# Gated cross-attention block with an expert router: VectorE turns the updated rows in 32x32 blocks, transfers within SBUF place them, and the batch chain runs a unit later

## The reference, cut to what matters

```
x = x + tanh(g_xattn) * attention(layernorm(x), ctx)     # Wq, Wk: 256x512, Wv: 256x512, Wo: 512x256
h = layernorm(x)                                         # over the 2048 positions of a row
logits = h @ router_weight.T + router_bias               # [rows, 2048] x [2048, 64]
scores = softmax(logits);  w, idx = top_k(scores, 8)
out = h * sum(w) + dense(w, idx) @ expert_bias           # [rows, 64] x [64, 2048]
x = x + tanh(g_ffn) * out
```

## Time and profile before

| | us |
|---|---|
| median of three runs | 1318.22 |
| lowest, highest | 1317.71, 1319.21 |
| span of the profiled execution (first to last instruction) | 1316.7 |
| TensorE products busy in it | 1273.2 |
| VectorE busy | 1004.8 |
| ScalarE busy | 893.3 |
| GpSimd busy | 712.7 |
| DMA queue of SyncE, share of the 16 engines | 27.7% |

### The profile page before, as it was taken

The page is one execution under the profiler, slowest core; times in us unless marked ns, Lnnn a source line. Parts: engine busy times, 40 slices in busy tenths (PEclk is TensorE's granted clock), DMA queues, the critical chain, the costliest instruction groups (busy, mean ns, idle before and its releaser), DMA issues.

```text
span 1316.7 us, 37880 instructions
## 1 busy us (share of the span) xinstructions
PE 1273.2 (97%) x15313; PEld 1120.4 (85%) x15313; DVE 1004.8 (76%) x1871; ACT 893.3 (68%) x1600; POOL 712.7 (54%) x662
## 2 busy tenths in 40 slices
PE   3999999999999999999999999999999999999997
PEld 3898888889878889798887899878888798888875
DVE  6669768896788966888678776888768797687677
ACT  4676667677686676766667776676676766686755
POOL 2655664556645665456663655636664556654531
PEclk9999999999999999999999999999999999999999
DMA  9331111811136111451115411153111721123103
GB/s 277 110 104 43 34 42 51 262 40 39 43 102 216 36 39 35 149 170 43 34 43 165 154 32 42 34 192 128 43 35 38 242 78 43 34 78 114 34 6 128
DMA packets 120620, 116.15 MB, mean 88 GB/s; under 512 B 11392, under 2 KB 88320, under 8 KB 120320
## 3 DMA queue, kind: packets, MB, share of 16 engines
q1 hardware_dynamic: 119584, 113.74, 27.7%
q10 hardware_dynamic: 864, 0.01, 0.0%
HBM read 80.06 MB, written 33.65 MB: 86 GB/s over the span
## 4 chain that ended last, share of the span: by engine, by line
PE 84%; DVE 7%; ACT 5%; issue 2%; DMA 1%; POOL 0%; SPq 0%; DVEq 0%; ACTq 0%; POOLq 0%
PE ring L316 9%; PE ring L317 8%; PE ring L318 8%; PE ring L436 5%; PE ring L392 4%; PE ring L403 4%; PE ring L438 4%; PE ring L437 4%; PE ring L355 4%; PE ring L331 4%; PE ring L332 4%; PE ring L333 4%; PE ring L417 4%; PE ring L451 4%; PE PR L463 3%; ACT X L720 2%
## 5 line engine op out<-in xcount | busy, mean ns | idle before, releaser
L316 PE MATMUL ring<-z_hi,wqk_hi 128*128 128x256 f32 x1024 | 297.1, 290 | 21.8 <-DVE z_lo L1029 21.8
L1128 POOL TENSOR_TENSOR cx_lo<-cx,cx_hi 128x512 fp32r<-128x512 f32 x128 | 165.9, 1296 | 262.7 <-ACT cx_hi L640 262.7
L317 PE MATMUL ring<-z_hi,wqk_lo 128*128 128x256 f32 x1024 | 290.5, 284 | 0.0
L318 PE MATMUL ring<-z_lo,wqk_hi 128*128 128x256 f32 x1024 | 290.3, 283 | 0.0
L316 PEld LDWEIGHTS ring<-z_hi,wqk_hi 128*128 128x128 f32 x1024 | 197.1, 193 | 32.8 <-DVE wqk_lo L1004 21.8
L851 DVE SCALAR_TENSOR_TENSOR xt<-ring,cst,mg 128x256 f32<-128x256 f32 x256 | 112.0, 478 | 144.2 <-PE ring L438 144.2
L1122 POOL TENSOR_TENSOR z_lo<-z,z_hi 128x1024 fp32r<-128x1024 f32 x62 | 148.5, 2394 | 134.7 <-ACT z_hi L624 134.7
L835 DVE RECIPROCAL o<-ring 128x512 f32<-128x512 f32 x64 | 214.1, 3345 | 0.4 <-PE ring L403 0.4
L317 PEld LDWEIGHTS ring<-z_hi,wqk_lo 128*128 128x128 f32 x1024 | 197.3, 193 | 0.0
L318 PEld LDWEIGHTS ring<-z_lo,wqk_hi 128*128 128x128 f32 x1024 | 197.2, 193 | 0.0
L1134 POOL TENSOR_TENSOR X<-X,xt 128x512 f32<-128x512 f32 x128 | 163.7, 1282 | 42.6 <-DVE xt L851 32.1
(11 more groups left out here) (154 smaller groups left out, 3032.1 us busy)
## 6 DMA issues: line engine op xcount, KB each, us to landing
cx<-in_ctx SPq DMA_DIRECT2D x128, 256.0 KB, 2.7
out_y<-X SPq DMA_DIRECT2D x128, 256.0 KB, 3.0
X<-in_x SPq DMA_DIRECT2D x112, 256.0 KB, 5.2
mg<-in_mask SPq DMA_DIRECT2D x64, 128.0 KB, 3.0
X<-in_x SPq DMA_DIRECT2D x8, 512.0 KB, 7.5
sel<-rows_d SPq DMA_DIRECT2D x256, 3.0 KB
X<-in_eb SPq DMA_DIRECT2D x2, 512.0 KB, 7.9
X<-in_wqT SPq DMA_DIRECT2D x1, 512.0 KB, 6.1
```

Of the source, the lines that this page charges most:

```text
L316: e.matmul(o, wqk_hi[:, t, cols], z_hi[:, t, :], t == 0, False)
L317: e.matmul(o, wqk_lo[:, t, cols], z_hi[:, t, :], False, False)
L318: last = e.matmul(o, wqk_hi[:, t, cols], z_lo[:, t, :], False, t == DT - 1)
L1128: e.tensor_tensor(cx_lo[:], cx[p % NC][:], f32(cx_hi[:]), ALU.subtract).then_inc(cxlo_g, 1)
```

## The change

The router's path takes another way for the first 61 units (`TF0 = TU - TURNED` = 61). `r_full` and hc are gone. `turn_h` (VectorE) transposes X itself, 128 x 1024 elements of a unit in blocks of 32x32, into `hq`; this leaves each block turned, but in the wrong place. `move_h` (SyncE) places the blocks with 16 transfers within SBUF, each of 32 partitions x 2 x 128 elements (32 KB), into `hT[u % 2]`. `r_high` reads hT (no bank), `r_low` moves from VectorE to GpSimd. For the last three units TensorE still transposes, now from X. Since the mean is no longer taken off before the turn, `c_base` takes the whole mean into the logits (dm = minus mean times the deviation's inverse). PR holds its columns in another order, which `c_logits` undoes while copying (`blocks`, `by_block`). The router's products stand later (`t_R` = 53.5 and 55.25 in place of `R` = 49.75 and 50), in the queue behind PV and DEN and behind MT; PV now stands ahead of DEN and so waits for the exponentials itself. The batch chain from `L` to the loads stands 16 slots (a unit) later for all batches but the last (`after`, `late` = 16). Statistics of the next batch stand at 73.5 + 1.25 i in place of 66.75 + 1.75 i. Most other slots and ends move by a little.

```
-    rows=-11.75, z32=-25.75, z_hi=-17.25, z_lo=-17.5, q=-11, q_ev=-12, k=-9, k_ev=-6.5,
-    c_hi=-13.25, c_lo=-10.5, v=-10, v_ev=-6.75, v_gap=-5,
-    S=0.5, top=2.75, split=5.75, MT=7.75, mt_ev=9.75, ST=12.75, exp=16.25, DEN=18.25, PV=20.75, rc=19, on=21,
-    gelu=24, mg=5, ot_hi=25.25, ot_lo=29.25, WO=30, WO_gap=1.5, xt=32, x1=35.25, bn2=39.5,
-    h=35.75, hT=39.75, hT_gap=0.25, ht_hi=42.25, ht_lo=44.5, R=49.75,
-    norm2=25.25, c_base=28.75, L=33.25, LT=36.75, c_top=35.5, c_exp=37.25, c_w=41.25, c_sc=42.75, wT=40.5, wt_hi=41.25, wt_lo=42.5, mix=44.5, m_gap=0.25,
-    sx=44.75, sx_gap=1.5, x2=46.5, rl=54.75, rl_gap=1,
-    x_1=10.0, x_gap=3.75, bn1=66.75, bn1_gap=1.75, norm1=96.75,
+    rows=-14.25, z32=-24, z_hi=-21.25, z_lo=-19.25, q=-10, q_ev=-11.75, k=-9, k_ev=-6.25,
+    c_hi=-14.5, c_lo=-10.5, v=-10, v_ev=-8.25, v_gap=-4.75,
+    S=1.25, top=2.75, split=5.75, MT=7.25, mt_ev=8.75, ST=10, exp=15, DEN=18.25, PV=17.75, rc=19, on=21.25,
+    gelu=21.25, mg=8.75, ot_hi=25.25, ot_lo=25.25, WO=30, WO_gap=1.75, xt=32.25, x1=36, bn2=40,
+    hT=38.5, hT_gap=0, ht_hi=47, ht_lo=44.75, R=43.5,
+    turn=36.25, move=40.5, t_hi=48.75, t_lo=46, t_R=53.5, t_gap=1.75, late=16,
+    norm2=27.75, c_base=34.5, L=25.75, LT=35.75, c_top=39, c_exp=37.5, c_w=41.25, c_sc=41.5, wT=41.25, wt_hi=43.75, wt_lo=43.5, mix=43.75, m_gap=0.25,
+    sx=45.5, sx_gap=1, x2=46.25, rl=48.25, rl_gap=1,
+    x_1=18.75, x_gap=3.75, bn1=73.5, bn1_gap=1.25, norm1=97.5,
...
+TURNED = 3
...
-        hc = [sb(f"hc{i}", [128, DT, U]) for i in range(2)]
+        hq = sb("hq", [128, 2, 4, DT * 32])
+        hT = [sb(f"hT{i}", [128, 2, D]) for i in range(2)]
...
+        def after(t, lag):
+            return due(t, 128 + lag + C["late"], 128, NB - 1) + tuple(b for b in due(t, 128 + lag, 128, NB) if b == NB - 1)
...
+        def blocks(ap):
+            return ap.rearrange("p (t a i) -> p a t i", t=DT, a=4)
+        def by_block(ap):
+            return ap.rearrange("p (a t i) -> p a t i", t=DT, a=4)
...
                 e.wait_ge(v_a, 2 * u + 2)
+                e.wait_ge(exp_a, 4 * (u + 1))
...
-                e.wait_ge(htlo_v, n + 1)
+                if u < TF0:
+                    e.wait_ge(htlo_g, n + 1)
+                else:
+                    e.wait_ge(htlo_v, n - 2 * TF0 + 1)
...
+            def move_h(u):
+                e.wait_ge(turn_v, u + 1)
+                if u >= 2:
+                    e.wait_ge(htlo_g, 2 * (u - 1))
+                for a in range(4):
+                    for q in range(4):
+                        e.dma_start(hT[u % 2][32 * q:32 * q + 32, :, a * 128:(a + 1) * 128],
+                                    hq[32 * a:32 * a + 32, :, q, :]).then_inc(hT_in[u % 2], 16)
...
-            def r_full(u):
-                b, c = divmod(u, NU)
-                if u >= 2:
-                    e.wait_ge(ht_pe, 2 * (u - 1))
-                if u < TU - 1:
-                    e.wait_ge(x1_g, 2 * (u + 1))
-                for t in range(DT):
...
+                if u < TF0:
+                    if a == 0:
+                        e.wait_ge(hT_in[u % 2], 256 * (u // 2 + 1))
+                    e.activation(ht_hi[a][:], hT[u % 2][:, a, :], ACT.Copy).then_inc(hthi_a, 1)
...
-                e.wait_ge(neg2_v, 2 * b + 1)
-                e.tensor_tensor(dm[:], ln2[:, 0, :], ln1[b % 2][:, 0, :], ALU.subtract).then_inc(dm_v, 1)
+            def turn_h(u):
+                if u:
+                    e.wait_ge(hT_in[(u - 1) % 2], 256 * ((u - 1) // 2 + 1))
+                b, c = divmod(u, NU)
+                e.wait_ge(x1_g, 2 * (u + 1))
+                e.transpose(hq[:].rearrange("p w q (t i) -> p (w q) t i", t=DT),
+                            X[b % 2][:, :, c * U:(c + 1) * U].rearrange("p t (c i) -> p c t i", i=32)).then_inc(turn_v, 1)
...
+            def r_low(u, a):
+                n = 2 * u + a
+                if u:
+                    e.wait_ge(r_pe, n - 1)
+                e.wait_ge(hthi_a, n + 1)
+                e.tensor_tensor(ht_lo[a][:], hT[u % 2][:, a, :], f32(ht_hi[a][:]), ALU.subtract).then_inc(htlo_g, 1)
```

More of the change, by code:

```diff
@@ L202, in gated_block_kernel @@
         gelu_a, othi_a, otlo_g, wo_pe, xt_v, x1_g = (sem(n) for n in ("gelu", "othi", "otlo", "WO", "xt", "x1"))
[L203 to L204 removed]
+        bn2_v, agg2_v, neg2_v, rstd2_g, ht_pe, hthi_a, htlo_v, htlo_g, r_pe = (sem(n) for n in (
+            "bn2", "agg2", "neg2", "rstd2", "hT", "hthi", "htlo", "htlo_g", "R"))
+        turn_v = sem("turn")
+        hT_in = [sem(f"hT_in{i}") for i in range(2)]
         l_a, lt_pe, dm_v, base_v, gate_v, lg_v, t8_v, neg_v, mr_v, sel_v, ex_a, w2_v, ac_v = (sem(n) for n in (
@@ L279, in gated_block_kernel @@
                 for u in units(t, "hT", C["hT_gap"] * a):
-                    take(("hT", 2 * u + a), t, end("ht_lo", u) - end("hT", u), htlo_v, 2 * u + a + 1)
-            for b in batch(t, C["LT"]):
+                    if u >= TF0:
+                        take(("hT", 2 * u + a), t, end("ht_lo", u) - end("hT", u), htlo_v, 2 * (u - TF0) + a + 1)
+            for b in after(t, C["LT"]):
                 take(("LT", b), t, C["c_top"] - C["LT"], lg_v, b + 1)
-            for b in batch(t, C["wT"]):
+            for b in after(t, C["wT"]):
                 take(("wT", b), t, C["wt_lo"] - C["wT"], wtlo_v, b + 1)
             for i in range(16):
-                for b in batch(t, C["mix"] + C["m_gap"] * i):
+                for b in after(t, C["mix"] + C["m_gap"] * i):
                     take(("mix", b * 16 + i), t, C["x2"] - C["mix"], x2_v, b * 16 + i + 1)
@@ L599, in _ @@
                     load_weight(u)
+                for u in due(t, C["move"], count=TF0):
+                    move_h(u)
                 for w in range(2):
@@ L604, in _ @@
                 for i in range(16):
-                    for b in batch(t, C["x2"] + C["m_gap"] * i):
+                    for b in after(t, C["x2"] + C["m_gap"] * i):
                         store(b, i // 4, i % 4)
-                    for b in batch(t, C["rl"] + C["rl_gap"] * i):
+                    for b in after(t, C["rl"] + C["rl_gap"] * i):
                         if b + 2 < NB:
@@ L1083, in _ @@
                     for u in units(t, "ht_lo", C["hT_gap"] * a):
-                        r_low(u, a)
+                        if u >= TF0:
+                            r_low(u, a)
+                for u in due(t, C["turn"], count=TF0):
+                    turn_h(u)
                 for b in batch(t, C["c_base"]):
                     c_base(b)
-                for b in batch(t, C["c_top"]):
+                for b in after(t, C["c_top"]):
                     c_top(b)
-                for b in batch(t, C["c_w"]):
+                for b in after(t, C["c_w"]):
                     c_weights(b)
-                for b in batch(t, C["wt_lo"]):
+                for b in after(t, C["wt_lo"]):
                     if b == NB - 1:
@@ L1094, in _ @@
                     w_low(b)
-                for b in batch(t, C["c_sc"]):
+                for b in after(t, C["c_sc"]):
                     if b < NB - 1:
@@ L1181, in _ @@
                         add_x(u, j)
+                for a in range(2):
+                    for u in due(t, C["t_lo"] + C["t_gap"] * a, count=TF0):
+                        r_low(u, a)
                 for b in batch(t, C["norm2"]):
```

67 lines of the change are left out of this document (36 added, 31 removed), and 10 rows, old and new, of the table ENDS.

## The result

The changed kernel takes 1514.76 us, the median of four runs (1511.91 to 1518.31). Against the kernel before, run beside it, that is a ratio of 1.1488, 95% interval 1.1474 to 1.1502: 196.5 us slower where 38 us less were forecast, and 205 us above the top of the range.

The account below looks back on a forecast made before the run. The prediction took TensorE's own work and order to bound the kernel: 1316.7 - 42.7 + 5 = 1279.0 us on the profiled span, 1280.5 with 1.5 for the median, stated as 1280. The range was 1262 to 1310.

Parts of the forecast that it names:

- the top of the range: Whole kernel: high bound 1310 us, from the late-VectorE rival's 1298 plus 6 and 6 for order and transfers.
- Steps 1 and 2: TensorE: eight transposes a unit leave in 61 units, 48.8 us; after reordering the net saving is 42.7 us.
- step 2: TensorE's order: router pairs stand apart, one more switch costs 0.1 us, net saving 0.70 us a unit, 42.7 in all.
- Step 3: VectorE's turn of 128x1024 takes 1.2 us; split ends 0.5 us before TensorE needs it, so few waits.
- Step 5: GpSimd takes two subtractions a unit, about 1.27 us each; v's waits for cx_lo stay near nothing.
- Step 6: Transfers on SyncE: issues 0.335 us each, ring 16.2 us against a 17.6 us unit; adds 5 us, bounds 0 and 18.
- Rival A: Ring of engines and transfers sets the pace: landing 5.2 us, 18.7 us a unit, 1343 us; chance 0.10.
- The step's own sign: ScalarE's ht_hi waits for the transfers a few us in all, against more than 50 us under Rival A.
- Step 7: Batch chain and statistics: no net change, bounds -9 and +14 us.
- Rival C: VectorE is late in the statistics and mix units, 2 to 3 us a batch: 18 more, 1298 us; chance 0.10.
- the allowance of 5: Transfers: about 1 us for an added unit of latency at two batches in three, 5 us in all.
- Rival B: VectorE and GpSimd shut each other out: split late 0.76 us a unit, 1326 us; chance 0.08, shared with a longer turn.

Follow-up runs that it names:

- e9: The changed kernel with e2's slots, c_base a unit later, statistics spread, the turn early and 16 transfers within SBUF: 1336.69 us, ratio 1.0138.
- e7: The changed kernel with five transfers a unit through DRAM (one write, four reads) in place of 16, same slots: 1403.85 us, ratio 1.067.
- e1: The changed kernel with eight of the 16 transfers a unit left out, so half of hT is stale: 1380.35 us in one run.
- e2: The changed kernel with four slots moved, so the next unit's x1 and turn no longer wait for this unit's transfers; all 16 kept: 1382.8 us, ratio 1.0487.
- e3: The changed kernel with TensorE transposing in all 64 units, no turn or transfers, router slots of before, other new slots kept: 1371.12 us, ratio 1.0395.
- e12: e3 with both the batch chain and the next batch's statistics back in their old slots: 1370.54 us, ratio 1.0387.
- e14: e12 with one slot changed, so the chain's exponential stands ahead of the next unit's gelu on ScalarE: 1367.07 us, ratio 1.0373.
- e8: The changed kernel with five transfers through DRAM, e2's slots, c_base a unit later, statistics spread and the turn early: 1334.27 us, ratio 1.0131.
- e4: A kernel that computes nothing, only series of eight transfers: 0.62 to 0.66 us an issue within SBUF, 0.31 to 0.46 from DRAM.

## Why the prediction was wrong

**Steps 1 and 2 hold.** 488 transposes are gone; a plain unit whose ring is short takes 17.53 us with TensorE busy in all of it (e9), forecast 17.5 to 17.7. In e9 the router's pairs stand together; apart, as in step 2, TensorE is busy 17.5 us in a plain unit too (e7), so no second switch shows.

**Step 3, the size holds, the place only half.** The turn takes 1.24 us (forecast 1.2), and in plain units split is in time. But the few waits of the turned maxima for split do not hold in the units with other VectorE work: 36.4 us in all in e9. The turn's group in the kernel after (busy us, mean ns of one, idle before and its releaser):

```profile
L916 DVE STREAM_TRANSPOSE hq<-X 128x1024 f32<-128x1024 f32 x61 | 75.5, 1238 | 155.8 <-POOL X L1177 155.8
```

**Step 5 nearly holds:** ht_lo is 1.28 us on GpSimd, and v waits 11.0 us in all for cx_lo, where near nothing was forecast.

**Step 6 is the step that failed.** Its term of 15 issues at 0.335 us was taken from four small transfers from DRAM. For transfers within SBUF an issue is 0.64: 10.7 us for 5.0. Rival A itself says that an issue of 0.47 would decide against the change, but neither the sum nor the range asks whether the row it was read from is of the same kind. The landing, on which rival A put its doubt, was better than assumed. Rival A (chance 0.10), "the ring of engines and transfers sets the pace", is what happened, by the term that its text names second; it was priced at 1343 us for a landing of 5.2, and never for a dearer issue. e1, e2 and e7 each remove the ring in another way (fewer issues, other slots, other transfers) and each brings plain units to 17.3 to 18.3. These removals bring 134, 132 and 111 us; the sum below takes the 132 of e2, which keeps all 16 transfers. The step's own sign, ht_hi's wait for the transfers, was 163.3 us as rival A had it, but does not tell by itself: in e9 that wait is 129.9 us and costs a plain unit nothing. The Trainium skill (DMA: Bandwidth & Descriptors, Rules for kernel authors) says to coalesce many small transfers, since under 64 KB one pays mostly overhead. The runs agree for 32 KB in a ring (16 issues 1514.8 us, five transfers 1403.9) and show that off it the overhead is hidden (1336.7 and 1334.3).

**Step 7 is the second.** Its "no net change" for chain and statistics, with an upper bound of +14, stands against 53 us by e3, with no turn in it. The statistics are 2 to 3 us a batch (the prediction saw 20 us of VectorE work in a 17.6 us unit and let the slack around take it; it doesn't). The mix unit is 3 us longer, and a plain unit 0.16. e12 and e14 show why no bound from one engine's sum was to be had in the mix unit: ScalarE's order of gelu, ex, scaled X and P, with the banks, sets it, and each wait removed came back at the next link. Rival C had this place with 18 us.

**The turn among that work** is the third: e2 is 11.7 us above e3, though its plain units are a microsecond shorter. With step 2's saving e3 less 42.7 would be 1328.4; e2 is 54.4 above that, and its waits for mxb are 61.2 us. (The saving beside e3 may be larger, 18.49 - 17.53 = 0.96 us a unit, and the loss with it.) e9 shows that much of this can be spread away, not all.

So the 235 us between forecast and result are 132 (ring) + 54 (turn and `c_base` among other VectorE work) + 53 (order), less the allowance of 5 that the forecast had for the transfers. These parts are differences of runs and the 42.7 of step 2, so they add up by construction; that each is one cause is not shown by the sum. The top of the range has a slip that decides nothing here: with step 6's own upper bound (18 in place of 5) it would be 1298 + 6 + 13 = 1317, not 1310.

**Rival B is there, beside the turn and not in it.** Durations of the first cast of the split (L823 before, L858 after: count, min/median/max ns), and VectorE rows with the GpSimd row of the same moment:

```profile
L823 DVE CAST mxb<-mx x64: 159/164/176, 39.2 to 1268.0; 128x16 bf16<-128x16 f32 x64
```

```profile
L858 DVE CAST mxb<-mx x64: 155/1002/1595, 39.0 to 1459.0; 128x16 bf16<-128x16 f32 x64
```

```profile
730.20 1.24 DVE L862 CAST mxb<-mr 128x16 bf16<-128x16 f32 x1
...
730.12 1.29 POOL L1171 TENSOR_TENSOR cx_lo<-cx,cx_hi 128x512 fp32r<-128x512 f32 x1 [0.19 <-ACT cx_hi L683]
```

```profile
638.29 2.64 DVE L970 TENSOR_TENSOR w<-ex,sc 128x512 f32<-128x512 f32 x1
...
637.87 2.51 POOL L1165 TENSOR_TENSOR z_lo<-z,z_hi 128x1024 fp32r<-128x1024 f32 x1
```

A cast of 16 elements takes 1.24 us and ends with GpSimd's cx_lo (731.44, 731.41); the weights take 2.64 us instead of 0.69, beside z_lo. The turn, which ran at 727.89 beside GpSimd's z, took its 1.25. The Trainium skill (SBUF — State Buffer, section on the two separate sides) says that a VectorE operation in a two-port mode or with two SBUF inputs locks the pair that it shares with GpSimd, or is shut out by it for the whole instruction. The weights, with two SBUF inputs, agree with it; the cast has one input and agrees only if it runs in a two-port mode, which no row shows. In the plain units it costs nothing that can be told: in e8 that cast's median is 936 ns, and a plain unit takes 17.53 us. In the slow units it is a part at most: in e2 the median is 210 ns and the loss is 64 us. The weights took 2.64 us at the median in the kernel after, in e1 and in e7, where TensorE waits some 44 us in all for them, and 0.69 in e9, where it waits 12; no run takes that away alone.

## What to carry to other kernels

Price an issue by a row of the same kind of transfer (within SBUF or from DRAM), and if there is none, bound it; then add up every closed loop of queues from the same stage to itself, since a loop longer than the unit sets the pace though no engine is full. Such a loop can be cut by a slot and not only by cheaper work: four slots gave 132 us, and fewer transfers on top of them nothing more. Steps of a batch chain that are placed by hand hold each other; moved one at a time they only pass the wait on, so a reordered stage needs its own count on each engine and of the banks, or it stays as it was.

## What was not expected of the hardware

A transfer within SBUF takes 0.62 to 0.66 us of SyncE's or ScalarE's queue to issue, for 16 KB as for 128 KB; one from DRAM 0.45 to 0.46, and 0.31 into three partitions (e4). One issue of a burst takes up to 1.45 us (714.86 in the chain above).

A tiny VectorE operation can pay most for its neighbour: the split's first cast went from 164 ns at the median to 1002 where it came to stand beside GpSimd's cx_lo, while the turn of 128x1024 stayed between 1.19 and 1.25 us in all 61 units.

Idle time cost TensorE a second time. In the stretches shown with long waits its granted clock is 0.86 to 0.93, a mean of the levels 2.4 and 1.2 GHz. In units without waits it is 1.00, and in some with them too (the plain one above, busy 18.59 of 21.08 us). Over the whole kernel after it is 0.948, and TensorE is busy 1277.5 us for 14825 products, where 15313 took 1273.2 at 0.999.
